# A graph network in one program: norms of two node updates moved by two steps, unread products on TensorE, one product moved from POOL to DVE

## Time and profile before

| | us |
|---|---|
| median of 3 executions | 4866.2 (4861.15 to 4872.02) |
| profiled execution | 4861.18 |
| its span, first to last instruction | 4859.4 |
| node update 0, steps | about 1237 to 1556 of the span |
| node update 1, steps | about 1906 to 2186 |
| node update 2, steps | about 2797 to 3555 |

### The profile page before, as it was taken

One profiled execution on the slowest core, in us unless ns is written; L12 is line 12 of the kernel. 1 busy time (PEld: TensorE's weight loads), 2 busy tenths in 40 slices (PEclk: granted clock), 3 DMA queues, 4 the chain that ended last, 5 costly groups with the idle time before them and its releaser, 6 DMA issues. The chain is left out here.

```text
span 4859.4 us, 52792 instructions
## 1 busy us (share of the span) xinstructions
PE 3140.8 (65%) x11864; PEld 1964.9 (40%) x11864; DVE 2736.5 (56%) x6239; ACT 913.0 (19%) x1645; POOL 2819.0 (58%) x2452
## 2 busy tenths in 40 slices
PE   4665746666897998664777568888736665555424
PEld 1223535555676887441222245555512222222113
DVE  7996742222455444665777627777756554444323
ACT  0332410000222000211222123333312221111100
POOL 0672057776110772556777578888247776887631
PEclk8875655555555555555555555555568887776655
DMA  6333621111564111442222344454211111332215
GB/s 257 73 72 118 263 83 24 24 24 21 131 166 133 26 26 35 168 173 81 41 42 41 54 58 80 94 96 94 60 54 36 37 36 32 32 30 28 24 14 109
DMA packets 337038, 363.08 MB, mean 75 GB/s; under 512 B 236961, under 2 KB 268844, under 8 KB 336865
## 3 DMA queue, kind: packets, MB, share of 16 engines
q1 hardware_dynamic: 219890, 261.52, 16.5%
q0 software_dynamic: 94096, 80.65, 13.8%
q10 hardware_dynamic: 22878, 18.95, 1.2%
HBM read 174.93 MB, written 201.00 MB: 77 GB/s over the span
## 5 line engine op out<-in xcount | busy, mean ns | idle before, releaser
L794 PE MATMUL e_ps<-e_msg,e_hot 128*128 x2408 | 571.4, 424 | 221.9 <-issue 211.9
L794 PEld LDWEIGHTS e_ps<-e_msg,e_hot 128*128 128x128 f32 x2408 | 530.1, 329 | 300.9 <-issue 300.9
L1762 POOL DMA_INDIRECT u_a<-attended,dst_end x392 | 482.0, 1230 | 148.0 <-issue 117.3
L2398 PE MATMUL d_pl<-d_hot,d_fields 128*65 128x512 f32 x712 | 479.8, 836 | 0.0
L767 DVE TENSOR_TENSOR sums<-e_ps,sums 128x455 f32 (+1 forms) x172 | 108.1, 629 | 556.0 <-PE e_ps L794 556.0
L712 POOL DMA_INDIRECT e_msg<-from_src,e_src x200 | 192.3, 962 | 288.7 <-DMA e_first<-lot_first 229.6
L1414 ACT ACTIVATE u_zt<-u_pt 128x256 f32<-128x256 f32 (+1 forms) x392 | 163.2, 432 | 867.3 <-PE u_pt L1314 867.0
L2342 POOL DMA_INDIRECT flows<-d_out,d_end x160 | 264.1, 1650 | 106.6 <-issue 104.1
L2053 POOL DMA_INDIRECT list<-s_rec,s_place x200 | 200.4, 1002 | 213.1 <-DVE s_place L1969 157.4
L2329 POOL DMA_INDIRECT d_near<-term,d_rec x196 | 190.9, 974 | 150.6 <-DMA d_rec<-list 91.1
L717 POOL DMA_INDIRECT e_msg<-h1d,e_src x200 | 205.0, 1025 | 115.0 <-issue 60.6
(11 more groups left out here) (379 smaller groups left out, 7478.1 us busy)
## 6 DMA issues: line engine op xcount, KB each, us to landing
x<-sums SPq DMA_DIRECT2D x28, 896.0 KB, 7.7
u_x<-x SPq DMA_DIRECT2D x28, 896.0 KB, 5.7
terms<-s_zeros SPq DMA_DIRECT2D x16, 812.5 KB
s_key_row<-src_key SPq DMA_DIRECT2D x50, 256.0 KB
term<-u_h SPq DMA_DIRECT2D x14, 910.0 KB, 3.7
flows<-s_zeros SPq DMA_DIRECT2D x14, 896.0 KB
n_x<-in_x SPq DMA_DIRECT2D x14, 896.0 KB
h<-n_h SPq DMA_DIRECT2D x14, 896.0 KB
```

What stands on the lines that cost most here:

```text
L794: last = nc.tensor.matmul(to, hot[s][:, q, :], rows, start=False, stop=q == LOT - 1)
L1762: pool.indirect_dma_start(A[s][:, j, :], None, net.attended[:, :], bass.IndirectOffsetOnAxis(ap=net.dst_end[:, tile:tile + 1], axis=0)).th ...
L2398: last = nc.tensor.matmul(pl[0:WEIGHT + 1, :], fields[:, j, :], hot[:, j, :], start=j == 0, stop=j == J - 1)
```

## The change

1. Updates 0 and 1: the norm of a step is spread over the two steps behind it. In step c, DVE does variance, scaling and last product of step c-2 (`old`) in sub-steps 0, 2 and 3, and sum and centring of step c-1 (`new`) in sub-steps 4 and 5. ACT makes the root of `old` after copy 1 and the squares of `new` after copy 6. The orders of SP's stores and of POOL in update 1 follow. Two rounds stand behind the last step instead of one.
2. `fill`: products of the bf16 identity with itself, 128x512, whose result nobody reads. Update 0: one after each sub-step and five at the start of each step, into a PSUM bank of their own. Update 2: one after each sub-step of `attend` and of `mlp`, four after the last of `mlp`, and four at the start of `mlp` behind its first two `turn`s. Update 1 has none.
3. Update 2: `TG` is made by DVE, in sub-step 3 of the next `attend`; POOL's product, its wait and DVE's wait for it go.

```diff
+def fill(nc, net, bank, count):
+    for _ in range(count):
+        nc.tensor.matmul(bank[:, :].rearrange("p (r c) -> p r c", c=P), net.identb[:, :],
+                         net.identb[:, :].unsqueeze(1).to_broadcast([P, J, P]), start=True, stop=True)
...
 # SP, update 1
-                        if before is not None:
-                            finish(before, hc)
+                        if old is not None:
+                            sp.wait_ge(normed, old[0] + 1)
+                            store_h(old)
+                            store_hc(old)
+                        if new is not None:
+                            sp.wait_ge(x_ready, new[0] + 1)
+                            store_x(new)
...
 # SP, update 0
-                            step(at(t, d), at(t, d + 2), at(t, d - 1))
+                            step(at(t, d), at(t, d + 2), at(t, d - 2))
...
 # TensorE, products (updates 0 and 2), mlp, and a step of update 0
                         last.then_inc(mm_done, 1)
+                        if layer != 1:
+                            fill(nc, net, unread if layer == 0 else pf[b][:, 0, :], 1)
...
                         last.then_inc(mm_done, 1)
+                        fill(nc, net, pf[b][:, 0, :], 1 if i < SUBS - 1 else 4)
                     turn(T[s], phase, 0, False)
                     turn(T[s], phase, 1, False)
+                    fill(nc, net, pf[(phase[1] + 1) % 2][:, 0, :], 4)
...
                         if layer == 0:
+                            fill(nc, net, unread, 5)
                             products(Z[c[1]], (c[0], c[1]), start)
...
 # ACT, updates 0 and 1
+                            if i == 1 and old is not None:
+                                root(old[0])
+                        if new is not None:
+                            square(new[0])
...
 # DVE, updates 0 and 1
-                    def norm_step(c, i):
-                        number, s, h = c
-                        if i == 0:
-                            total(summed(number))
-                        elif i == 1:
-                            centre(summed(number))
-                        elif i == 3:
-                            variance(number)
...
+                    def norm_step(new, old, i):
+                        if i == 0 and old is not None:
+                            variance(old[0])
+                        elif i == 2 and old is not None:
+                            if layer == 0:
+                                scale_twice(old)
+                            else:
+                                v.wait_ge(stored_h[old[1]], 16 * h_stores * old[2])
+                                scale(H[old[1]][:, :, 0:C], old[0], relu=True).then_inc(normed, 1)
+                        elif i == 3 and old is not None:
+                            if layer == 0:
+                                begin_sums(old)
+                            else:
+                                row_means(old)
+                        elif i == 4 and new is not None:
+                            total(summed(new[0]))
+                        elif i == 5 and new is not None:
+                            centre(summed(new[0]))
...
                     for i in range(SUBS):
-                        norm_step(at(0, LAST), i)
+                        norm_step(at(0, LAST), at(0, LAST - 1), i)
+                    for i in range(SUBS):
+                        norm_step(None, at(0, LAST), i)
...
 # DVE, update 2
+                            if t is not None and i == 3:
+                                v.drain()
+                                nc.vector.tensor_tensor(TG[t[1]][:, :, :], T[t[1]][:, :, :], channels(net.norms[:, 0, :]), ALU.mult)
...
-                                if i == 0:
-                                    v.wait_ge(tg_ready, c[0] + 1)
                                 evacuate(c, phase, i, 1)
...
 # POOL, update 1
                     with pool.Fori(0, SUPER // 2 - 2) as t:
-                        for d in (1, 2):
-                            less_mean(at(t, d - 1))
+                        for d in (2, 3):
                             joined(at(t, d + 2))
-                            biased(at(t, d))
+                            less_mean(at(t, d - 2))
+                            biased(at(t, d - 1))
...
 # POOL, update 2
-                    for d in range(SUPER):
-                        gained(at(0, d))
-                        if d + 2 < SUPER:
-                            gather(at(0, d + 2))
+                    for d in range(2, SUPER):
+                        gather(at(0, d))
```

More of the change, by code:

```diff
@@ L1230, in _, with step @@
                 if layer == 1:
[L1231 to L1241, removed]
+                    def step(c, after=None, new=None, old=None):
+                        if c is not None:
+                            sp.wait_ge(inputs_used, c[0] + 1)
                         if after is not None:
                             load(after)
-                        if before is not None:
-                            finish(before, hc)
+                        if old is not None:
[5 more added lines that the diff above has]
+                            store_x(new)
                     step(at(0, 0), at(0, 2))
@@ L1439, in _, with step @@
                 if layer < 2:
-                    def step(c, before=None):
+                    def step(c, new=None, old=None):
                         for i in range(SUBS):
[L1442 to L1447, removed]
+                            copy((c[0], c[1]), i, new is None)
+                            if i == 1 and old is not None:
+                                root(old[0])
+                        if new is not None:
+                            square(new[0])
                     if layer == 0:
@@ L1450, in _ @@
                     step(at(0, 0))
+                    step(at(0, 1), at(0, 0))
                     with act.Fori(0, SUPER // 2 - 1) as t:
-                        for d in (1, 2):
-                            step(at(t, d), at(t, d - 1))
-                    step(at(0, LAST), at(0, LAST - 1))
+                        for d in (2, 3):
+                            step(at(t, d), at(t, d - 1), at(t, d - 2))
+                    root(LAST - 1)
                     square(LAST)
@@ L1593, in step, with row_means @@
+                    def row_means(c):
+                        s = c[1]
+                        v.drain()
+                        nc.vector.tensor_reduce(h_mean[s][:, :], H[s][:, :, :], AX.X, ALU.add)
+                        v.drain()
+                        nc.vector.scalar_tensor_tensor(h_mean[s][:, :], h_mean[s][:, :], 1.0 / C, one[:, :], ALU.mult, ALU.mult).then_inc(meant, 1)
+                    def step(c, new=None, old=None):
                         v.wait_ge(loaded[c[1]], 16 * in_loads * (c[2] + 1))
@@ L1595, in step @@
                             evacuate(c, (c[0], c[1]), i, 0)
-                            if before is not None:
-                                norm_step(before, i)
+                            norm_step(new, old, i)
                         v.drain()
@@ L1730, in less_mean @@
                                                 ALU.subtract).then_inc(hc_ready, 1)
[L1731 to L1733 removed]
+                    for d in range(4):
+                        joined(at(0, d))
                     biased(at(0, 0))
                     with pool.Fori(0, SUPER // 2 - 2) as t:
[L1736 to L1737 removed]
+                        for d in (2, 3):
                             joined(at(t, d + 2))
[L1739 to L1745 removed]
+                            less_mean(at(t, d - 2))
+                            biased(at(t, d - 1))
+                    for d in range(LAST - 1, LAST + 2):
+                        less_mean(at(0, d - 2))
+                        biased(at(0, d - 1))
                     less_mean(at(0, LAST))
                 else:
[L1748 to L1754 removed]
                     def gather(c):
```

54 lines of the change are left out of this document (14 added, 40 removed).

## The result

| | before | after |
|---|---|---|
| median (lowest to highest), us | 4866.2 (4861.15 to 4874.55), 5 runs | 4835.18 (4793.24 to 4841.47), 5 runs |
| profiled execution | 4861.18 | 4793.24 |

The ratio of the times is 0.9903, 95% interval 0.9877 to 0.993: faster by about 1%. The five times lie in two groups, 4793 and 4802 at a granted clock of 0.649 and 0.644 over the whole span, and 4835 to 4841 at 0.630 to 0.637. The profiled execution is the fastest of them, 42 us under their median, so the same kernel was profiled again (`again`, among the experiments). None of the three long executions was profiled.

What follows compares the result with a forecast made beforehand. Bounds: TensorE in update 0, a DVE-ACT-TensorE chain in update 1, POOL's gathers and product in update 2. Terms -33 - 18 - 16 - 4 = -71 on 4861.2 gave 4790, 4795 on medians; 8-in-10 range 4755 to 4865 us.

Steps and rivals of the forecast that it cites:

- Part 1: Update 2: POOL's product moved to DVE cuts POOL's step from 48.8 us by 2.7, -33 us in all (-48 to -23).
- the tail: Update 2 behind the last gather: two MLP phases, -18 us in sum, 15 of it if TensorE's clock is up.
- the +1.24 us of the new product: Update 2: DVE's new product holds up POOL's gathers by 1.24 us a step (bounds 0 and 2.03).
- 46.1: Update 2: POOL's predicted step in us, 48.8 - 3.97 + 1.24, if TensorE and DVE fit in it.
- the fourth rival: Update 2: moving the product does nothing, another limit stands right behind POOL's; gains there shrink to -15, 4831 us; chance 4%.
- Part 3: Updates 0 and 2: unread products cost 0.43 or 0.22 us each and pay only by raising TensorE's clock, expected to rise.
- with the MLP phase at the upper one: Update 2: at the upper clock the MLP phase falls from 28 us to about 18 to 20, so TensorE fits.
- Part 4: Updates 0 and 1: norms over two more steps; update 1's long centrings get short, steps 19.6 us, -16 us (-20 to +9).
- the bare round: End of updates 0 and 1: one more round of norm work with nothing beside it, 7 to 9 us.
- Update 0 (-4): Update 0: clock up for half the sub-steps, steps of 22.3 us; -5, -7 and +8 sum to -4 (-35 to +60).
- The first rival: Updates 0 and 2: the clock stays down and every unread product is bare cost, +92 us, 4958 us; chance 10%.
- the third: Rival for update 0: the clock is up throughout it, -30 us there, 4769 us in all; chance 12%.

Runs made afterwards that it cites:

- again: The changed kernel unchanged, run and profiled once more: 4823.15 us, ratio 0.9918.
- product_only: The kernel before with only POOL's product of update 2 moved to DVE: 4838.9 us, ratio 0.9943.
- no_fill: The changed kernel without any unread products, norms and moved product kept: 4826.18 us, ratio 0.9923.
- product_twice: `product_only` with DVE making the moved product twice in each step, same values written again: 4871.1 us, one execution.
- late_fill: The changed kernel with unread products only in update 2's MLP phases: eight behind the opening wait, one after each sub-step but the last: 4814.22 us, ratio 0.9892.
- norms_only: The kernel before with only the norms of updates 0 and 1 spread over two steps, no unread products: 4846.33 us, ratio 0.996.
- late_fill_and_0: `late_fill` with update 0's unread products put back as in the change: 4797.06 us, ratio 0.9856.

## Why the prediction was right, and where it was not

*Part 1, POOL's product (-33).* `product_only` gives -28 in update 2, against -33 and the 3.5 of the tail that need no clock. The product holds gathers up as said, but the sum is mis-sized, and the limit is another. Mean gather 1301 ns before, 1309 in `no_fill`, 1306 in `product_only`: 0.1 to 0.2 us more per 28 and not 1.24. The term mis-sized is the +1.24 us of the new product. In the order of time `no_fill` shows the mechanism (DVE's product, and the gather that ends 0.8 us behind it):

```profile
2976.70 2.02 DVE L1524 SCALAR_TENSOR_TENSOR u_xc<-u_mean,u_y 128x1792 f32<-128x1792 f32 x1
2977.40 2.15 POOL L1767 DMA_INDIRECT u_a<-attended,dst_end  x1 [0.30 <-issue]
...
2979.15 2.02 DVE L1666 TENSOR_TENSOR u_tg<-u_t,norms 128x1792 f32<-128x1792 f32 x1
2979.85 2.14 POOL L1767 DMA_INDIRECT u_a<-attended,dst_end  x1 [0.30 <-issue]
```

In the stretches of ten steps shown (`no_fill`, `product_twice`), gathers over 1.1 us are 79 of 280 before, 91 of 291 in `no_fill` and 94 of 285 in `product_twice`; DVE products of 128x1792 with both operands in SBUF that begin there are 79, 90 and 94. Each of the long gathers overlaps one of them. So it is about one gather for each product, as the prediction had it. But each is held up for less (in the mean 1.26 us over the median of 0.947 before, 1.16 in `no_fill`, 1.13 in `product_twice`), so most of the addition is given back; no experiment shows why. All the same POOL's 45.2 us, 28 x (1.309 + 0.305), were not reached: DVE and TensorE do not fit in 46.1 without the clock, where the prediction had added DVE's busy time (32.4 us) and left out the waits between the two engines. That is the fourth rival's mechanism, at 46.7 us, and worth 2.2 instead of 2.7 us a step.

*Part 3 and update 2 with the clock.* Where the clock is up in the MLP phase, the step is POOL's: after 28 x (1.327 + 0.305) = 45.7 by the gathers and 45.2 measured in the mean, predicted 46.1; TensorE 77% busy (345.79 of 451 us, 2914 to 3365); clock 0.78 there and 0.72 in `late_fill`. The mean gather of 1327 ns, and 1341 in `late_fill`, against the predicted 1330 to 1360 is luck: the prediction took its rise from DVE's product, which alone gives 1306 to 1309, and the rest came with the unread products, no run says how. Update 2 in all: -48.3 in the profiled execution, -51 by the sum. The step that failed is "with the MLP phase at the upper one": it took the rise as given in every phase. `again` has nine phases of 14 in which it does not come, and steps of 49.1 us; five of them stand behind a wait of over 2 us for ACT's copy. `again`'s 26 us more in update 2 are of the size of what its own median lacks to the 4795. That the long executions of the change lack it for the same reason is inferred from their lower clock (0.630 to 0.637), not seen.

*Part 4, update 1 (-16).* -17.6; in the other kernels with the new order, -13 to -22. The mean centring fell to 2.40 us, not to 2.03, and the steps from 19.6 and 22.1 in turn to 19.3. From TensorE's last product of the update to the next stage it is 37.4 us where it was 29.5: the bare round of the prediction's 7 to 9 us. In the order of time, after:

```profile
1979.02 3.19 POOL L1746 TENSOR_TENSOR u_hc<-u_h,u_h_mean 128x1792 f32<-128x1792 f32 x1 [6.94 <-DVE u_h_mean L1605]
1981.67 2.42 DVE L1524 SCALAR_TENSOR_TENSOR u_xc<-u_mean,sums 128x1792 f32<-128x1792 f32 x1
1984.30 3.97 POOL L1739 TENSOR_TENSOR sums<-sums,norms 128x1792 f32 x1 [2.08 <-DVE u_xc L1524]
1988.22 3.19 POOL L1734 TENSOR_TENSOR sums<-sums,dinv  x1
```

The centring now begins when POOL's subtraction is nearly over (it ends at 1982.21), and POOL's next two products lie behind it.

*Update 0 (-4).* -4.0 and -10.0, steps of 21.7 to 24.8 us, clock 0.75: right, and for the reason given (up at the burst, a hole of 3.17 us, down). Its terms, taken apart: from TensorE's first product of the update to its last it is 13.5 us shorter than before (-12 was predicted, the first two steps in it), and from there to the next stage 30.5 us instead of 21.9 (+8 was predicted). Without additions the rotation costs 6 to 7 in all (`norms_only` +6.6, `no_fill` +6.1); the additions bring 5 to 19 (from 359 to 362 without them to 343 to 354). Neither pays alone: rotation alone 360, additions alone 369, both 343 to 354, neither 353 to 357.

*The numbers.* The median lies in the range (4755 to 4865) and 10 us beyond the forecast's own (4770 to 4825), in which `again`'s lies. By the medians 31 us were gained where 71 were forecast, and by the time alone the result can't be told from the fourth rival's 4831. That the profiled execution (4793) lies next to the forecast is luck of the draw. As `no_fill` and `again` show, the norms and the moved product account for what the median gained, and the clock, to which the sum gave 15 us in the tail and the room to reach POOL's 46.1 us a step, for nothing measurable. The first rival was excluded by the clock, the third (up throughout update 0) by steps of 24.8 us. What the prediction lacked is a case between "up" and "down" in update 2. With the 756.6 us of `again` for that stage in place of 730.6, the profiled execution of 4793 would have been 4819.

## What to carry to other kernels

Put an instruction that is there to bring the clock up directly in front of the phase that is to be fast, behind the last wait of that phase. Four kernels that do so, with eight of them, had the clock up in every such phase; four ahead of the wait had it in 18 phases of 28. The place and the number were not tried apart. When work is taken from an engine that is never idle, ask for the length of the next chain with its waits in it, not for the busy time of its engines: here it stood at about the same 48.8 us. And where an edit gains only in some steps, one profiled execution can be far from the median (here 42 us): profile it twice.

## What the runs showed of the hardware

*POOL and DVE.* A DVE operation with both operands in SBUF that begins while POOL's product runs ends 1.88 us behind POOL's end: the earlier trace rows 2047.70 and 2049.58; after, 1982.21 and 1984.09; and 1.89 in the earlier trace rows. Its 2.02 us thus all but begin anew. It goes the other way too. In every second step of update 1 before, DVE begins 0.08 us ahead of POOL. DVE then takes its 2.03 us (2066.89 in the earlier trace rows), and POOL's product takes 4.99 us in place of 3.19:

```profile
2066.97 4.99 POOL L1717 TENSOR_TENSOR sums<-sums,dinv  x1
```

So the steps of 22.1 and 19.6 us in turn are those in which DVE and in which POOL is the one held up. The Trainium skill, "SBUF — State Buffer", Who interferes with whom, says that such a DVE operation contends with a GpSimd one that reads SBUF, and that the order of issue decides which of the two is blocked. The cases of update 1 agree, in both directions. In the earlier trace rows DVE had begun 0.42 us before POOL and was held up all the same, as in ten more steps of update 2. The same section infers that a tensor_tensor does not hold up the writing of descriptors by GpSimd; here the gathers that start during one (in `no_fill`, above) last 2.15 and 2.14 us, where the median before was 0.947, and all 79 gathers over 1.1 us in the ten steps before overlap a DVE product with both operands in SBUF (of the 201 shorter ones 49 do).

*The spread.* Within the five runs of the change the time goes with the mean granted clock (0.649 at 4793 us, 0.630 to 0.637 at 4835 to 4841). That kernels whose clock is up only in some steps scatter more is not shown: the change has 48 us over five runs, and the same kernel 13 us over five in `again`; `no_fill` has 15 over five, `norms_only`, at a clock of 0.596 to 0.604, 28 over eight, and before 23 over thirteen. `late_fill_and_0` still scatters (21 us over four), and its ratio lies 0.6% under `again`'s.
